# Graph network with expert layer: expert weights requested in two parts from the end of the second gather, and a reordered ScalarE slot

## What is computed

```python
x = x + gnn0(layernorm(x), src, dst, edge_weight, W, b)          # segment_sum of gathered rows
x = x + ffn0(layernorm(x))                                       # top-k routed
x = x + gnn1(layernorm(x), edge_weight1, weight, gate_weight)    # per relation and edge, relu
gate_logits = xf @ Wg + bg
top_w, top_i = top_k(gate_logits, 2); top_w = softmax(top_w)
for e in range(8):
    h = gelu(xf @ W1[e] + b1[e])
    out = out + w_dense[:, e:e+1] * (h @ W2[e] + b2[e])
```

## Time and profile before

| | |
|---|---|
| runs | 4001.47, 4003.86, 4015.01 us |
| span of the profiled execution, first to last instruction | 3402.6 us |
| median less span: what lies around the span | 601.3 us |
| PE busy | 2615.4 us (77%) |
| DVE busy | 1733.1 us (51%) |
| ACT busy | 723.6 us (21%) |
| POOL busy | 1869.7 us (55%) |
| DMA, mean over the span | 128 GB/s |

### The profile page before, as it was taken

One profiled execution on the slowest core, in us unless ns is written; L12 is line 12 of the kernel. 1 busy time (PEld: TensorE's weight loads), 2 busy tenths in 40 slices (PEclk: granted clock), 3 DMA queues, 4 the chain that ended last, 5 costly groups with the idle time before them and its releaser, 6 DMA issues. The chain is left out here.

```text
span 3402.6 us, 59974 instructions
## 1 busy us (share of the span) xinstructions
PE 2615.4 (77%) x14271; PEld 1921.6 (56%) x14272; DVE 1733.1 (51%) x5663; ACT 723.6 (21%) x1907; POOL 1869.7 (55%) x1915
## 2 busy tenths in 40 slices
PE   7688888887777799999655555564555389999997
PEld 6577777776665344444344444443444267767774
DVE  6455545454554655555355454544544544545553
ACT  4121111111110233333211010000000233333332
POOL 1777777777774000000377777777777245555554
PEclk9899999998999899999888888777777689999998
DMA  7333333333332444444545454555544623222232
GB/s 224 110 113 113 113 111 111 113 113 113 110 113 67 173 197 192 188 191 194 194 141 155 151 154 142 152 154 151 146 146 146 241 59 48 45 45 48 45 48 33
DMA packets 175589, 434.08 MB, mean 128 GB/s; under 512 B 41712, under 2 KB 103792, under 8 KB 169232
## 3 DMA queue, kind: packets, MB, share of 16 engines
q0 software_dynamic: 97072, 236.21, 26.9%
q1 hardware_dynamic: 57424, 183.78, 14.1%
q10 hardware_dynamic: 21008, 13.24, 1.3%
HBM read 275.05 MB, written 158.04 MB: 127 GB/s over the span
## 5 line engine op out<-in xcount | busy, mean ns | idle before, releaser
L776 POOL DMA_INDIRECT g_msg<-table,idx x1564 | 1517.3, 970 | 518.8 <-issue 476.5
L848 PE MATMUL psum<-g_msg,g_hot 128*128 x3328 | 967.4, 456 | 593.0 <-SPq L719 358.1
L848 PEld LDWEIGHTS psum<-g_msg,g_hot 128*128 128x128 f32 x3328 | 756.5, 233 | 789.5 <-issue 654.5
L796 DVE TENSOR_SCALAR g_hot<-iota,g_cols 128x128 f32<-128x128 f32 x1664 | 450.1, 364 | 31.9 <-DVE g_cols L793 30.5
L1908 POOL DMA_INDIRECT out<-ex_y,ex_to x112 | 206.0, 1839 | 253.9 <-DMA out<-ex_y,ex_to 165.3
L768 POOL MEMSET g_origin<- 128x256 f32 x1 | 0.3, 313 | 590.8 <-POOLq L1359 590.8
L1594 PE MATMUL psum<-wrel_halves,t_xhi 128*128 128x512 f16 x784 | 298.2, 380 | 1.7 <-DVE t_row L1475 1.7
L1595 PE MATMUL psum<-wrel_halves,t_xhi 128*128 128x512 f16 x784 | 298.1, 380 | 0.0
L1596 PE MATMUL psum<-wrel_halves,t_xlo 128*128 128x512 f16 x784 | 298.1, 380 | 0.0
L1475 DVE TENSOR_SCALAR t_row<-psum,t_gate 128x256 f32<-128x256 f32 x392 | 171.2, 479 | 233.7 <-PE psum L1596 231.7
L2074 PE MATMUL psum<-w,ex_ghi 128*128 x784 | 260.6, 382 | 6.7 <-DVE ex_y L1983 6.4
(11 more groups left out here) (353 smaller groups left out, 3231.7 us busy)
## 6 DMA issues: line engine op xcount, KB each, us to landing
table<-t_row SPq DMA_DIRECT2D x48, 2048.0 KB, 6.3
g_msg<-table,idx POOLq DMA_INDIRECT x1564
piece_stage<-in_w SPq DMA_DIRECT2D x32, 512.0 KB, 5.7
w_halves<-piece_halves SPq DMA_DIRECT2D x32, 512.0 KB, 3.4
w<-w_halves SPq DMA_DIRECT2D x8, 2048.0 KB, 22.6
rows<-sc_row ACTq DMA_DIRECT2D x50, 128.0 KB, 2.2
out<-acc ACTq DMA_DIRECT2D x49, 128.0 KB
table<-t_row SPq DMA_DIRECT2D x24, 256.0 KB, 2.5
```

The costliest lines, as they stand in the source:

```text
L776: pool.indirect_dma_start(out=msg[:, at:at + D], out_offset=None, in_=table, in_offset=bass.IndirectOffsetOnAxis(ap=t[f"idx{g}"][:, n:n + ...
L796: last = nc.vector.tensor_scalar(hot[b][:, k * P:(k + 1) * P], t["iota32"][:, :], c3[:, k, where:where + 1], c3[:, k, weight:weight + 1], ...
L848: pe.matmul(ps, hot[b % PAIR][:, k * P:(k + 1) * P], msg[:, bass.ds(slot_at[k], D)], start=False, stop=False, skip_group_check=True).then_ ...
```

## The change

**The load in two parts.** `load_experts` now gives two functions. `begin` is issued by SP as soon as it is through with the second gather's own work and 48 of the 49 windows are stored. It takes the pieces whose whole SBUF place lies in the first 48 windows of `acc` or of `side`: 12 + 3 pieces of W1 and 8 of W2, 23 of 32, in six transfers, then both biases. `end` has the other 9 pieces, in three transfers, behind the waits that stood before the whole load. For the count of 48, `scalar_first` now adds 16 to `x_stored`, so that the first threshold is reached one store earlier.

**The ACT slot.** `Score.scalar` copies the transposed tile first. The wait for the landing of the row store, the high half of the row and the store to `out` come second, and the store to `out` now waits for the landing of the one before it.

**Register work.** `slot_number` and the number of a closed window are read with `value_load` with bounds, and three counts on PE are masked with 1023.

```diff
     def slot_number(eng, m):
-        _, (n,) = nc.values_load_multi_w_load_instructions(slot_at(m, 0, 1), engines=[eng.engine], min_val=0, max_val=WINDOWS,
-                                                           skip_runtime_bounds_check_because=sure)
-        return n
+        return eng.value_load(slot_at(m, 0, 1), min_val=0, max_val=WINDOWS)
...
-                    pe.wait_ge(tiles_in, code[MSG_TILES])
+                    pe.wait_ge(tiles_in, code[MSG_TILES] & 1023)
...
-                            pe.wait_ge(bank_free, code[BATCH + k // BANKS] + 1)
+                            pe.wait_ge(bank_free, (code[BATCH + k // BANKS] & 1023) + 1)
...
-                    _, (n,) = nc.values_load_multi_w_load_instructions(
-                        t["closed"][0:1, bass.ds(m, 1)], engines=[act.engine], min_val=0, max_val=WINDOWS - 1 - k,
-                        skip_runtime_bounds_check_because=sure)
+                    n = act.value_load(t["closed"][0:1, bass.ds(m, 1)], min_val=0, max_val=WINDOWS - 1 - k)
...
+        act.sem_inc(self.core.x_stored, 16)
...
         self.store(act, n, bass.ds(last * P, P))
-        hold(act, "act", self.stored, 16 * n)
-        hold(act, "act", self.norm.done, n)
-        nc.scalar.activation(self.row[:, 0:D], self.xn[:, :], ACT.Copy, scale=X_SCALE).then_inc(self.hi_done, 1)
-        act.dma_start(self.out[bass.ds(begun * P, P), :], tile_of(self.t["acc"], begun)).then_inc(self.core.x_stored, 16)
         hold(act, "act", self.turned, n + 1)
         nc.scalar.activation(self.xT[:, :], self.psT[:, 0:D], ACT.Copy).then_inc(self.xT_done, 1)
+        hold(act, "act", self.stored, 16 * n)
+        nc.scalar.activation(self.row[:, 0:D], self.xn[:, :], ACT.Copy, scale=X_SCALE).then_inc(self.hi_done, 1)
+        hold(act, "act", self.core.x_stored, 16 * n)
+        act.dma_start(self.out[bass.ds(begun * P, P), :], tile_of(self.t["acc"], begun)).then_inc(self.core.x_stored, 16)
...
         sp.dma_start(self.table[:, :], self.dram["place_table"]).then_inc(self.consts_in, 16)
+        sp.wait_ge(self.core.x_stored, 16 * WINDOWS)
+        self.load[0](sp)
         sp.wait_ge(self.score.out_done, WINDOWS + self.score.LAST)
         sp.wait_ge(self.score.stored, 16 * (WINDOWS + 1))
-        sp.wait_ge(self.core.x_stored, 16 * WINDOWS)
-        self.load(sp)
+        sp.wait_ge(self.core.x_stored, 16 * (WINDOWS + 1))
+        self.load[1](sp)
...
+    gone = [(places["acc"], places["acc"] + 4 * (WINDOWS - 1) * D), (places["side"], places["side"] + 4 * (WINDOWS - 1) * D)]
+    inside = lambda at: any(a <= at and at + bytes_of <= b for a, b in gone)
+    early = [[n for n in range(own) if inside(base + n * bytes_of)] for base in (first, second)]
+    rest = [[n for n in range(own) if n not in some] for some in early]
```

More of the change, by code:

```diff
@@ L20 @@
+import itertools
 from contextlib import ExitStack
@@ L2095, in _, with load_experts, load, begin @@
             slots(pe, slot)
[L2098 to L2108, removed]
+def load_experts(core, dram, w1, w2, b1, b2, places):
+    own = Pieces.count
+    piece = 2 * H
+    first, second = places["w1"], places["w2"]
+    bytes_of = 2 * piece
+    gone = [(places["acc"], places["acc"] + 4 * (WINDOWS - 1) * D), (places["side"], places["side"] + 4 * (WINDOWS - 1) * D)]
+    inside = lambda at: any(a <= at and at + bytes_of <= b for a, b in gone)
+    early = [[n for n in range(own) if inside(base + n * bytes_of)] for base in (first, second)]
+    rest = [[n for n in range(own) if n not in some] for some in early]
+    runs = lambda ns: [list(g) for _, g in itertools.groupby(ns, key=lambda n: n - ns.index(n))]
+    PART = 4
+    parts = lambda ns: [run[k:k + PART] for run in runs(ns) for k in range(0, len(run), PART)]
+    def load(sp, some):
+        for to, view, ns in ((w1, dram["w1_halves"], some[0]), (w2, dram["w2_halves"], some[1])):
+            for part in parts(ns):
+                a, n = part[0], len(part)
+                sp.dma_start(to[:, a * piece:(a + n) * piece].rearrange("p (n d) -> p n d", n=n),
+                             view[a:a + n].rearrange("n p d -> p n d")).then_inc(core.experts_in, 16)
+                core.experts_loads += 1
+    core.experts_loads = 0
+    def begin(sp):
+        load(sp, early)
+        sp.dma_start(b1[:, :], dram["b1_1"]).then_inc(core.experts_in, 16)
+        sp.dma_start(b2[:, :], dram["b2_1"].partition_broadcast(P)).then_inc(core.experts_in, 16)
+        core.experts_loads += 2
+    def end(sp):
+        load(sp, rest)
+    return begin, end
 def program(nc, dram, out):
@@ L2161, in program @@
         w1 = w.sb("w1_1", [P, EXPERTS * KC * H * 2], F16)
+        places["w1"], places["w2"] = experts_free, w.at
         w2 = w.sb("w2_1", [P, EXPERTS * HC * D * 2], F16)
@@ L2173, in program @@
         keep = Work(core, w.at + GATHER_BYTES)
-        placed = Place(core, t, keep, late, follow, dram, lambda sp: load_experts(core, sp, dram, w1, w2, b1, b2))
+        placed = Place(core, t, keep, late, follow, dram, load_experts(core, dram, w1, w2, b1, b2, places))
         gather(core, t, dram["table1"], 1, t["side"], w.at, pieces, follow, placed)
```

## The result

| | before | changed |
|---|---|---|
| runs | 4009.44 us, median of 4 (4001.47 to 4018.53) | 4054.03 us, median of 4 (4047.20 to 4060.86) |
| ratio | | 1.0108 [1.0086, 1.0131] |
| profiled execution: time, span | span 3402.6 us | 4060.86 us, span 4059.0 us |

The account below looks back on a forecast made before the run. The prediction took POOL's fetches to bound both gathers, so only what follows a last fetch could move. Its terms, -0.7 + 1.1 + 2.1 = +2.5 us on 4003.86, gave 4006.4 us, range 4000 to 4014.

Parts of the forecast that it names:

- Around the span 601.3 us stay: Whole run: 601.3 us of the run time lie outside the profiled span of 3402.6 us and don't change.
- the ring of slots never held POOL back: Both gathers: before its fetches POOL is idle almost only for its own 0.3 us of issue.
- a gather lasts its 782 fetches: Both gathers: 782 fetches by 0.970 + 0.305 us set the length, some 997 us each.
- work on PE, ACT or DVE inside it costs nothing until PE falls a ring behind: Inside a gather: added work is hidden; in the first, PE waited 63.3 us in all for arrivals.
- Rival 3: First gather: PE becomes the bound if a reading costs 1 us, not 0.3; 4016 us or more, chance 0.05.
- Weights earlier: Behind the second gather: starting the already hidden load earlier saves no wait for weights, gain by itself 0.
- Facts' store: End of Place: with weights down at 2713 it lands near 2720, hidden behind the DVE chain; -0.7 us.
- Register work: End of the first gather: three readings by 0.3 us and 0.2 for masks delay PE, and DVE with it; +1.1 us.
- Row store beside weights: End of the second gather: landing takes 4.4 us instead of 1.8 beside weights, so the last logits come 2.1 us later.
- the upper end: Row store's landing: 3.5 us without a packet, 1.2 for its rows, 0.6 for completion; 5.4 us, logits +3.1.
- 128 / 103 = 1.2 us: Row store's landing: its 128 rows, served one for one with weights at 2058 in 20 us, take 1.2 us.
- Copy first: ACT's slot after the second gather: copy at 2676.3 instead of 2677.00, gain kept only if the row store lands early.

Follow-up runs that it names:

- reg_only_2: The kernel before with the change's register work alone, at the 4010 us pace: 4047.36 us, ratio 1.0095 [1.0061, 1.0129] against the kernel before.
- dve_act_pad: The changed kernel with three more checked readings of each slot number on DVE and ACT, none on PE: 4147.41 us, 1.0352 of the kernel before.
- reg_only: The kernel before with the change's register work alone, at the 3402 us pace: 3401.04 us, ratio 0.9998 [0.9989, 1.0007] against the kernel before.
- after_again: The changed kernel unchanged, run again at the 3402 us pace: 3405.70 us, ratio 1.0011 [1.0002, 1.0021] against the kernel before.
- order_late_load: The changed kernel with all weights behind the old waits, at the 3402 us pace: 3402.10 us, ratio 1.0001 [0.9992, 1.0010] against the kernel before.
- pe_pad: The changed kernel with two more register instructions on PE for each of 1664 product steps: one run, 4316.72 us, the kernel before 4012.29 beside it.

## Why the prediction was wrong

**The step that failed** is "Around the span 601.3 us stay". A difference of 601.3 us between a span and its run times was taken for something outside the kernel. It was inside: the runs were of another pace than the profile. What was read from that profile for the timed runs, that "the ring of slots never held POOL back", that a gather lasts its 782 fetches, and that "work on PE, ACT or DVE inside it costs nothing until PE falls a ring behind", holds at 3402 us and fails at 4010 us, where the forecast was asked for, as the profiles of the changed kernel and of `reg_only_2` show. With 651.7 us of ring waits instead of none, the price of register work is not 1.1 us but 38.3 (`reg_only_2`).

**Rival 3** had the direction: instructions in the gathers, not the two edits that the change is about. Its mechanism was too narrow. It looked at PE's room in the first gather; at the 4010 us pace readings on DVE and ACT cost as well (`dve_act_pad`), in both gathers, and its size, 36 us added on PE, fits the result only by chance, since the condition that it named (the room of 63.3 us used up) is not what decided.

**The terms, at the pace of the profile.** The forecast there was +2.5 us; +3.6 was measured. That the two are close is partly luck: the row store's term was 2.8 us short, and the 1.1 us at the first gather's end was not there.

- *Weights earlier, 0*: right. No weight was waited for in either kernel.
- *Facts' store, -0.7*: right. It lands 16.5 us after its issue instead of 29.9, and the time from the logits to the experts falls by 0.9 us. Its cover is now the DVE chain:

```profile
rows<-facts ACTq DMA_DIRECT2D x1, 100.0 KB, 16.5
...
2731.22 0.22 DVE L1787 CAST node_to<-pl_none 128x112 int32<-128x112 f32 x1
...
2732.08 1.28 ACT L2025 ACT_TABLE_LOAD   x1 [5.65 <-PEq L711]
```

- *Register work, +1.1*: the times can't tell. `reg_only` is 0.9998, and its interval reaches from -3.7 to +2.4 us. Where the prediction put the cost there is none: PE did come 1.0 us late to L1055 behind the first gather, but the second down product then took 1.99 us instead of the 2.77 of the earlier trace rows, and from the last fetch of this gather to the first of the next it is 592.0 us (before 592.5). Behind the second gather there is one: `reg_only` issues the row store 4.46 us after its last L869, before 3.78 after L871, and has the logits 0.9 us later (8.92 against 8.01). The first gather's end in `after_again`:

```profile
1071.03 3.72 PE L847 MATMUL psum<-g_msg,g_hot 128*128 x16 [2.07 <-SPq L724]
1075.72 3.69 PE L1055 MATMUL psum<-w,f_g 128*128 128x256 f32 x16 [0.98 <-issue]
...
1085.33 1.99 PE L1055 MATMUL psum<-w,f_g 128*128 128x256 f32 x8 [2.12 <-ACT f_g L1031]
```

- *Row store beside weights, +2.1*: the mechanism was right, the size was not. The landing took 7.6 us where 4.4 was taken and 5.4 was the upper end, and L870 to the logits rose by 4.9 us. The step that was short is "128 / 103 = 1.2 us", the rows one for one with weights. Of the upper end's three parts, the 3.5 us without a packet were 3.6 and the 0.6 for the completion 0.66, but the store's records took 3.3 us (2674.15 to 2677.46); alone, in the earlier trace rows, the first came after 0.86 us and the last 0.5 us later. The rule of the Trainium skill ("DMA: Bandwidth & Descriptors", section "Queues, rings and completion order") that was worked out beside it gave a wait of 1.4 to 2.7 us. The trace agrees so far as its first record came 2.7 us later than alone; that the rows would then go together, as the prediction went on, it does not bear out.
- *Copy first*: the forecast gave it no gain of its own. Without weights beside it, it gives 1.6 us on the way to the logits (7.29 in `order_late_load` against 8.92 in `reg_only`), of which the late facts' store takes back 1.4 (55.12 against 53.75). Beside them it gives 1.35 us there (12.94 against 14.29).

**What stays open.** Why this program runs at the one pace or the other, and whether that goes by chip. How the 38.3 us divide between masks and checked readings: of the 1260 instructions that the register work adds (59974 to 61234 in the two profiles), 632 are on PE, and at the 0.077 us of `pe_pad` these alone would cost an estimated 49 us, within the interval of the whole cost (25 to 52 us), so PE's part may be all of it or only some. And the kernel before itself was not profiled at the 4010 us pace; of its runs there only the spans are known.

## What to carry to other kernels

Before anything is read from a profile, hold its span against the run times: here the two are 2 us apart in every execution whose both numbers are known, so a difference of 600 us says that profile and times are of different conditions, and no "this engine never waits" may be carried from the one to the other. Where POOL issues indirect DMAs by the hundred, register work in the loops of the other engines may be hidden at one pace of the program and cost 38 us at another, as here; masks and checked readings are worth moving out of the loop even when the profile at hand shows cover for them. And a store on which a serial chain waits should land before a bulk load is started on another queue: here weights asked for 12 us earlier (6.1 us behind the last fetch instead of 17.7), which nobody waited for, held a row store back for which the whole of Place waited, and made the way to the logits 5.65 us longer (12.94 against 7.29) and the kernel 3.6.

## What the runs showed of the hardware

While POOL issues indirect DMAs, the other engines get their instructions in fits at the 4010 us pace: matmuls with all operands at hand start 1.43, 2.78, 2.11, 2.79 and 1.41 us apart, all near a multiple of 0.70 us. It is not more code to be loaded. The list of DMA queues has nearly the same instruction records (q14) at both paces: 69 in the changed kernel at 4010 us and 68 at 3402 us, 0.56 MB each. From 200 to 900 us it has 6 of them, while PE was idle 134 times inside the up product alone.

The Trainium skill, "Runtime: NRT & Kernel Launch", section "Instruction fetch mechanics", says that instructions are fetched ahead in sequence, in blocks of 256, and that this stays hidden unless a taken branch leads out of the two blocks that are held. There is no branch among the 32 matmuls, so by that page the holes would not be the fetch, and the 6 records for 134 holes agree. In what way POOL's indirect fetches hold the instructions up no run here shows.

The holes fall on register instructions too, on DVE, ACT and PE alike. The line view of the checked slot readings (L686; count, ns min/median/max, first and last start) has this for the last of their instructions in the changed kernel at 4010 us:

```profile
L686 DVEq SEQ_ASSERT  x108: 15/23/1393, 94.8 to 3313.3; - x108
L686 ACTq SEQ_ASSERT  x108: 4/18/708, 115.8 to 3326.5; - x108
L686 PEldq SEQ_ASSERT  x108: 3/18/704, 119.4 to 3323.2; - x108
```

and at 3402 us:

```profile
L686 DVEq SEQ_ASSERT  x108: 23/23/41, 93.0 to 2652.4; - x108
L686 ACTq SEQ_ASSERT  x108: 18/18/23, 100.8 to 2668.7; - x108
L686 PEldq SEQ_ASSERT  x108: 18/18/26, 102.4 to 2665.7; - x108
```

The medians are the same. The longest took 0.70 or 1.39 us, once or twice the step of the holes between the matmuls. A median hides this pace altogether; the maximum and the idle time for "issue" show it. An instruction more on PE costs 255.9 us / 3328 = 0.077 us there on the mean (`pe_pad`, one run).
